# Row transposes one slot later, last roots on VectorE, two expert tiles turned inside the last diffusion tile, some high halves on ScalarE

## The reference

```
a   = layernorm(x)
h   = silu(a @ W_in.T + b_in)
out = term = h
for i in 1..6:                       # diffusion
    term = segment_mean(term[src], dst) / i
    out  = out + term
x1  = x + out @ W_out.T + b_out
xn  = layernorm(x1) * gamma + beta
lg  = xn @ Wr + br                   # 8 logits of a row
w   = softmax(top 2 of lg)
y   = sum over the 2 chosen experts e of
      w_e * (gelu(xn @ W1[e] + b1[e]) @ W2[e] + b2[e])
result = x1 + y
```

## Time and profile before

| | us |
|---|---|
| median of 3 runs (1249.70 to 1251.24) | 1250.63 |
| the profiled execution | 1251.38 |
| its span | 1249.6 |
| sixth step and its row work | 860.1 to 1026.1 |
| expert stage on TensorE | 1029.3 to 1217 |
| TensorE busy in the span | 1154.7 (92%) |
| VectorE, ScalarE, GpSimd busy | 722.2, 414.0, 221.7 |

### The profile page before, as it was taken

One profiled execution on the slowest core, in us unless ns is written; L12 is line 12 of the kernel. 1 busy time (PEld: TensorE's weight loads), 2 busy tenths in 40 slices (PEclk: granted clock), 3 DMA queues, 4 the chain that ended last, 5 costly groups with the idle time before them and its releaser, 6 DMA issues.

```text
span 1249.6 us, 26380 instructions
## 1 busy us (share of the span) xinstructions
PE 1154.7 (92%) x7843; PEld 817.3 (65%) x7843; DVE 722.2 (58%) x1504; ACT 414.0 (33%) x810; POOL 221.7 (18%) x272
## 2 busy tenths in 40 slices
PE   5798999999999999999999999999999977899990
PEld 3586766676566666666666666665666656899980
DVE  7888999993443334442354334442456667866655
ACT  1675665661000000000122111210132227567653
POOL 3000000000112111212000000000022136666750
PEclk8998999999999999999999999999999989999995
DMA  6111010014344334433243123322143232222367
GB/s 158 49 49 30 26 34 30 21 40 104 83 92 111 74 84 99 94 87 64 83 141 109 42 88 98 103 74 32 43 138 113 79 115 76 79 82 91 95 167 214
DMA packets 76860, 105.99 MB, mean 85 GB/s; under 512 B 13472, under 2 KB 62423, under 8 KB 76651
## 3 DMA queue, kind: packets, MB, share of 16 engines
q1 hardware_dynamic: 63044, 72.45, 19.4%
q0 software_dynamic: 11376, 25.55, 9.1%
q10 hardware_dynamic: 2356, 6.93, 2.2%
HBM read 77.00 MB, written 37.49 MB: 92 GB/s over the span
## 4 chain that ended last, share of the span: by engine, by line
PE 78%; DVE 11%; DMA 4%; issue 3%; DVEq 2%; ACT 2%; POOL 1%; ACTq 0%; SPq 0%; POOLq 0%
PE ps L1937 43%; PE ps L1988 8%; PE ps L1915 7%; PE ps L2094 5%; PE ps L2108 5%; PE ps L1883 4%; DVE v_b L1178 4%; PE ps L1851 1%; DMA h_ring<-h_dram 1%; DMA y_dram<-adj,v_a 1%; PE ps L1862 1%; PE ps L2069 1%; DMA adj<-y_dram 1%; DVE adj L1085 1%; PE ps L2031 1%
## 5 line engine op out<-in xcount | busy, mean ns | idle before, releaser
L1937 PE MATMUL ps<-v_a,adj 125*125 125x512 f16 x1375 | 297.3, 379 | 0.0
L1937 PE MATMUL ps<-v_b,adj 125*125 125x512 f16 x1250 | 270.2, 379 | 2.2 <-DVE v_b L1203 2.2
L1937 PEld LDWEIGHTS ps<-v_a,adj 125*125 (+1 forms) x1375 | 187.6, 136 | 109.0
L1937 PEld LDWEIGHTS ps<-v_b,adj 125*125 x1250 | 170.6, 136 | 101.6 <-issue 2.6
L895 ACT ACTIVATE t_hi<-ps,cinv 125x256 f32<-125x256 f32 x125 | 59.2, 474 | 460.1 <-PE ps L1937 404.1
L1185 DVE SCALAR_TENSOR_TENSOR t_hi<-ps,cinv,t_hi 125x256 f32<-125x256 f32 x125 | 60.4, 483 | 240.8 <-ACT t_hi L895 240.8
L1178 DVE TENSOR_TENSOR v_b<-v_b 125x2560 f16<-125x2560 f16 x125 | 180.3, 1488 | 7.7 <-PE ps L1883 7.1
L1988 PE MATMUL ps<-v_b,adj 125*125 125x512 f16 x625 | 143.7, 388 | 3.0 <-DVEq L1371 3.0
L870 ACT ACTIVATE adj<-ps 125x625 f32 (+1 forms) x125 | 112.2, 906 | 67.4 <-PE ps L1883 66.5
L1915 PE MATMUL ps<-v_a,adj 125*125 125x512 f16 x500 | 124.0, 381 | 0.0
L1988 PEld LDWEIGHTS ps<-v_b,adj 125*125 125x125 f16 x625 | 85.4, 140 | 51.5 <-issue 3.7
(11 more groups left out here) (298 smaller groups left out, 1004.4 us busy)
## 6 DMA issues: line engine op xcount, KB each, us to landing
h_ring<-h_dram SPq DMA_DIRECT2D x125, 125.0 KB
v_a<-L_ffn_W SPq DMA_DIRECT2D x32, 256.0 KB, 3.3
v_b<-L_ffn_W SPq DMA_DIRECT2D x32, 256.0 KB, 3.3
adj<-w_dram SPq DMA_DIRECT2D x16, 512.0 KB, 5.4
w_dram<-w_hi SPq DMA_DIRECT2D x32, 128.0 KB, 1.9
hx_dram<-h_dram POOLq DMA_DIRECT2D x25, 125.0 KB, 2.6
hx_dram<-x POOLq DMA_DIRECT2D x25, 125.0 KB, 3.2
hx_dram<-L_gnn_b_out POOLq DMA_DIRECT2D x25, 125.0 KB, 4.1
```

The source lines that it names most:

```text
L1937: last = te.matmul(ps[0:NP, u, :], of_tile(adj[0:NP, 0:ADJ], i, u, a * NP, NP), source[:, a, :], start=(a == 0), stop=(a == T - 1))
```

## The change

It has six parts.

1. Row tiles are transposed on TensorE in slot w+2 in place of w+1, save tiles 10 to 14, which stay; logits follow a slot later on TensorE and on VectorE. Transposes of tiles 23 and 24 and logits of 22 to 24 stand behind the sixth step.
2. TensorE's wait for `term_ok` goes into the untaken branch. Tile 0 waits in its place until 24 of the 25 input tiles are written, and its 25th matmul for the last one.
3. The roots of row tiles 15 to 19 are taken in slot 19, ahead of `place_a`; in slot 20 GpSimd writes the iotas ahead of `add_beta`. Both were in the other order, the roots in slot 20.
4. The roots of tiles 20 to 24 are computed on VectorE alone behind the sixth step (`group_of_itself`, three iterations from an integer first guess), in place of a square root in slot 24 and another for the last tile. The Gelu table is loaded in slot 22.
5. Gathers 0 to 2 are issued in slot 24 ahead of `add_beta` of tile 19; expert tiles 0 and 1 are transposed ahead of matmuls 15 and 20 of the last diffusion tile, and tile 2 behind the hidden part of tile 0. Scaling of row tiles 20 to 24 on ScalarE moves behind Gelu 0 and Gelu 1.
6. For expert tiles 6 to 16 the high half is written by ScalarE behind the Gelu.

```diff
+    HH_TILES = range(6, 17)
...
+        TURN_AT = (T - 10, T - 5)
+        def turn_slot(w):
+            return w + 1 if TA - WIN <= w < TA else w + 2
+        def turned_in(m):
+            return [w for w in range(T) if turn_slot(w) == m]
+        def turn_bank(j):
+            return 2 if j == 0 else (j - 1) % 2
... GpSimd
-                if has(5):
-                    add_beta(m - 5, u)
                 if m == T - 5:
...
+                if m == T - 1:
+                    for r in range(WIN):
+                        pool.wait_ge(xs_out[r], 16 * (TA // WIN))
+                    pool.wait_ge(S["idx_ok"], 1)
+                    for j in range(3):
+                        gather(j)
+                if has(5):
+                    add_beta(m - 5, u)
...
-            for j in range(5):
+            for j in range(3, 5):
                 gather(j)
             add_beta(T - 5, 0)
... ScalarE, the sixth step
-                if m == T - 1:
-                    root_of(NB, WIN - 1)
                 if has(5):
                     normalised(m - 5, u, i)
+                if m == T - 1:
+                    transposed(0)
+                    transposed(1)
...
-                if has(1):
-                    transposed_rows(m - 1)
-                if has(5) and m < T - 1:
+                for w in turned_in(m):
+                    transposed_rows(w)
+                if has(5):
                     high_rows(m - 5, u, i - 1)
...
+                if m == T - 3:
+                    a.activation(gb_max, gb_max, ACT.Gelu)
... ScalarE, expert tile j
                 last.then_inc(S["gelu_ok"], 1)
+                if j in HH_TILES:
+                    act.wait_ge(S["gelu_ok"], j + 1)
+                    need(act, S["ffn_y"], j - FR + 1)
+                    a.activation(h_hi[j % FR]..., h_g[r], ACT.Copy, scale=sh[...]).then_inc(S["hh_ok"], 1)
             def between(j):
                 if j == 0:
-                    normalised(T - 4, 1, NB)
-                    normalised(T - 3, 2, NB)
+                    for k in range(3):
+                        normalised(T - WIN + k, k, NB)
...
-            transposed(0)
-            high_rows(T - 6, 4, NB - 2)
-            normalised(T - 5, 0, NB)
-            act.wait_ge(S["ve_ok"], NB + 1)
-            a.activation(sd3, ve3, ACT.Sqrt).then_inc(S["sd_ok"], 1)
-            transposed(1)
-            a.activation(gb_max, gb_max, ACT.Gelu)
-            transposed_rows(T - 1)
-            transposed(2)
+            transposed_rows(T - 2)
... VectorE
-                if has(3):
-                    logits(m - 3)
-                if has(1):
-                    statistics2(m - 1)
+                for w in turned_in(m - 2):
+                    logits(w)
+                if has(1) and m != T - WIN:
+                    row_statistics(m - 1)
-                if u == 0 and has(WIN):
+                if u == 0 and has(WIN) and m < T - WIN:
                     group_scales(m - WIN, WIN, i)
-                if m == T - 1:
-                    group_scales(T - WIN, WIN - 1, NB)
...
                 if m == T - 6:
+                    row_statistics(m)
+                    group_scales(m + 1 - WIN, WIN, NB - 1)
                     place_a()
...
+            def group_of_itself(t0):
+                group = slice(t0, t0 + WIN)
+                v.tensor_scalar(ve2, mv2[:, group, 1], 1 + 1e-5, 1e-5 ** 2, ALU.mult, ALU.add)
+                v.drain()
+                v.tensor_scalar(root_i, ve2.bitcast(I32), 1, None, ALU.logical_shift_right)
+                v.tensor_scalar(half2, ve2, -0.5, None, ALU.mult)
+                v.drain()
+                v.tensor_scalar(sd2.bitcast(I32), root_i, -1.0, float(0x5f3759df), ALU.mult, ALU.add)
+                v.drain()
+                for _ in range(3):
+                    v.tensor_tensor(rt2, sd2, sd2, ALU.mult)
+                    v.drain()
+                    v.tensor_tensor(rt2, rt2, half2, ALU.mult)
+                    v.drain()
+                    v.scalar_tensor_tensor(sd2, rt2, 1.5, sd2, ALU.add, ALU.mult)
+                    v.drain()
+                group_rows(group, sd2)
... VectorE behind the sixth step
-            statistics2(last)
-            ...
-            logits(last - 2)
+            logits(last - 3)
+            row_statistics(last)
+            group_of_itself(T - WIN)
             low_rows(last - 5, 4)
-            dve.wait_ge(S["sd_ok"], NB + 1)
-            newton(v, sd3, ve3, rt3)
... VectorE, hidden(j)
+                if j in HH_TILES:
+                    dve.wait_ge(S["hh_ok"], HH_TILES.index(j) + 1)
+                else:
+                    dve.wait_ge(S["gelu_ok"], j + 1)
...
-                v.tensor_scalar(hh, h_g[r], sh[:, bass.ds(e, 1)], None, ALU.mult)
-                v.drain()
+                if j not in HH_TILES:
+                    v.tensor_scalar(hh, h_g[r], sh[:, bass.ds(e, 1)], None, ALU.mult)
+                    v.drain()
... TensorE
-            pe.wait_ge(S["term_ok"], 1)
-            pe.wait_ge(S["psum_read"], LAST + 5)
+                pe.wait_ge(S["term_ok"], 1)          # inside the branch that isn't taken
...
                     pe.wait_ge(S["psum_read"], n + 4)
+                    if m == 0:
+                        pe.wait_ge(S["v_ready"], T * STEPS - 1)
                     for a in range(T):
+                        if m == 0 and a == T - 1:
+                            pe.wait_ge(S["v_ready"], T * STEPS)
+                        if m == T - 1 and a in TURN_AT:
+                            transposed(TURN_AT.index(a))
...
-                if has(1):
-                    transposed_rows(m - 1)
+                for w in turned_in(m):
+                    transposed_rows(w)
...
-                if has(2):
-                    logits(m - 2)
+                for w in turned_in(m - 1):
+                    logits(w)
... TensorE, ffn_tiles
-            transposed(0)
+            transposed_rows(T - 2)
...
-    transposed(1)
...
-            if b == 0 and j + 2 < count:
+            if b == 0 and 0 < j < count - 2:
                 transposed(j + 2)
             if j < count:
                 hidden(j, b, *entries[j])
+            if b == steps - 1 and j == 0:
+                transposed(2)
```

## The result

| | before | after |
|---|---|---|
| median, us | 1250.16 (1248.67 to 1251.24) | 1240.83 (1239.4 to 1241.85) |
| ratio, 95% interval | | 0.9921 (0.9908 to 0.9935) |
| span of the profiled execution | 1249.6 | 1239.5 |
| end of step five's matmuls | 857.14 | 858.51 |
| transposes of expert tile 14 | 1079.23 | 1069.17 |

The account below looks back on a forecast made before the run. TensorE was taken to bound the kernel, so only its gaps and clock count. Terms -3.2 -1.1 -2.0 -4.9 -2.6 +0.44 -4.9 +0.7 -1.4 sum to -19.0; from 1251.38 that gives 1232.4, forecast 1232 us, range 1228 to 1240.

Parts of the forecast that it names:

- Seam: Start of the sixth step: 1.6 us idle for the branch's instruction fetch, tile 2 starting 3.2 us earlier.
- the case of a free fetch: At the seam: if the instruction fetch cost nothing, `pool_const` would hold tile 2 at 869.4.
- Tile 6 and the later transposes: Sixth step: later transposes shrink stalls caused by VectorE; after tile 6, 1.39 us becomes 0.3, -1.1.
- Slots 19 to 24: Sixth step: reordered VectorE and GpSimd work gives -2.0 at tile 22, -4.9 at tile 23, -2.6 by full clock.
- Rival (a): Slots 19 to 22: GpSimd's iotas hold VectorE, 2.7 us at most, clock 2.6 more: 1235 to 1237 us; chance 0.10.
- No idle over 2.8 us is left, so tile 23 runs at full clock: -2.6: Tile 23 of the sixth step: without long idles ahead, its matmuls keep full clock, saving 2.6 us.
- Entry and split: Into the expert stage: gathers hidden, first split 6.8 us behind tile 24's end, -4.9 new.
- idle of 3.2: Expert tile 1: TensorE idle from about 1021.5 until VectorE's logits at 1024.7, 3.2 us.
- rival (b): The clock falls anyway, at the seam or in expert tile 1: 1234 to 1237 us; chance 0.12.
- The last line of the ledger: From the first split to expert tile 14: -0.7 us, from +0.7 for Gelu 1 and -1.4 for the high halves.
- the ledger: Forecast against measured gains from step five's end to expert tile 14, line by line: -19.0 forecast, -11.4 measured.
- 1.5 at the seam: Tiles 0 and 1 of the sixth step: 1.5 us lost to low clock before, expected to be regained.

Follow-up runs that it names:

- positions_spread: The changed kernel with two of the three groups of `positions` (20 of 30 narrow matmuls) moved between the matmuls of tile 23: 1263.48 us, 0.9914 of the kernel before.
- early_turns: The changed kernel with rows 0 to 9 transposed one slot earlier, as before the change: 1270.86 us, 0.9956 of the kernel before.
- direct18: The changed kernel with the statistics of row tile 18 written in place, without the small copy: 1235.88 us, 0.9898 of the kernel before.
- betas_wait: The changed kernel with every tile's statistics written in place and GpSimd's work on tiles 15 and 16 behind `place_a`: 1261.04 us, 0.9905 of the kernel before.
- place_positions: `betas_wait` with two of the three groups of `positions` moved between the matmuls of tile 23: 1234.89 us, 0.9877 of the kernel before.
- best3: `place_positions` with logits copies of tiles 22 and 23, gathers 3 to 7 and last weights load earlier, high halves from expert tile 2: 1230.08 us, 0.9843.

## Why the forecast was half right

- **Seam, right in size, wrong in place.** -3.2 forecast, -3.1 measured. The idle of 1.6 us that I had put down to the branch's fetch isn't there (858.51 follows the last matmul at once; two instruction fetches, at 855.89 and 859.60, ran beside matmuls), and `pool_const` holds 1.46, which I had named as the case of a free fetch. By the Trainium skill, "Runtime: NRT & Kernel Launch", section "Instruction fetch mechanics", a taken branch stalls if its target isn't in the fetched window; whether it was, no run shows, and the largest idle at this place in any trace with this seam is 0.21 us (`positions_spread`).
- **Tile 6 and the later transposes**: 1.39 to 0.33, as forecast; `early_turns` shows that without them 1.9 us of the seam's 3.1 would be lost at tile 0's x1.
- **Slots 19 to 24: the failed step.** The sentence "the sum of VectorE's work up to the low half of tile 20 is unchanged, only its waits go" fell. The work moved beside GpSimd's. Rival (a) was this mechanism, priced at 2.7 at most and given 0.10, by the iotas alone. I left out that GpSimd's two-input work on tiles 15 and 16 also moved beside `place_a`, and that VectorE's two-input operations took 0.58 to 0.64 us beside it, for 0.17 to 0.28. `direct18` and `betas_wait` give 1.34 and up to 1.45, so tile 22 came at +0.2 and not at -2.0. The other 2.2 at tile 23 are 1.7 of clock in tile 22, and 0.5 for `positions`: the sum took 2.0 for it, but it took 2.55 (1003.67 to 1006.22), as it had before the change (1008.90 to 1011.44).
- **"No idle over 2.8 us is left, so tile 23 runs at full clock: -2.6"** fell twice. An idle of 3.06 was left, and the clock fell at tile 23 with none ahead of it. Behind 1.48 us of idle in `direct18` it also fell, at 991.6, while before it had not behind 2.77: idle length is not the condition I took it for.
- **Entry and split, right.** The first gather is issued 3.9 us ahead of tile 24's start (1010.03 for 1013.89; 1.2 to 2.8 ahead were forecast), there is no wait for the gathers, and the first split comes 7.1 us behind the end of tile 24 (6.8 forecast).
- **Expert tile 1**: the idle of 3.2 was 4.03, and rival (b) came true, 6.8 us at low clock, so that Gelu 2 was late and VectorE waited 2.23 for it (1034.80). The last line of the ledger, which also has the high halves, is +0.2 for -0.7.
- **Together**, the 7.6 us missing in the ledger are 2.2 at tile 22, whose cause, the contention, is shown; 3.4 of low clock in tiles 22 and 23 (7.30 and 7.26 us for 5.59), measured, though why the clock falls just there is only in part shown; 0.5 for `positions`; and some 1.4 from the first split on, not taken apart. The clock was to give back 4.1 (2.6 at tile 23, 1.5 at the seam) and gave back nothing in sum: 17.0 us low before, 17.0 after. `place_positions`, which removes the contention and spreads `positions` and nothing else, has a stretch of 207.7 where the forecast's was 203.1, as new waits take their place in the entry. `best3` gets to 201.8, but with four more edits.
- **The rivals were priced one at a time.** (a) and (b) came true together. With the added times that I gave them, 3 to 5 and 2 to 5 us, that is 1237 to 1242 (an estimate), and the range ended at 1240.

## What to carry to other kernels

When VectorE work is moved, list what GpSimd does in the same microseconds: here one small copy out of SBUF was held for 1.34 us and operations on two SBUF inputs took two to three times as long, and a chain of them was 2.4 to 2.8 us longer. Count clock falls as a balance and not as a price of one idle time, and over more than one trace; breaking up a block of 30 narrow matmuls kept the clock in slots 21 to 24 in two programs where removing the idle had not in three. Waits in a stage with several lagging engines cover each other: the idle of 4.03 taken out alone gave 1.1, the contention alone 1.1, all the edits together some 9.

## What the runs showed that I had not expected

- A copy of 125 x 2 fp32 on VectorE took 1.51 us beside a GpSimd iota whose row names no input (0.17 alone), in ten traces of ten.
- In three programs the clock fell for 3.4 us behind 30 matmuls of 44 columns, with no idle over 0.45 us in slots 21 to 23.
- Two traces of one program had their first five falls between 300 us and expert tile 8 at the same instructions, and then differed; programs that differ in a few instructions had them elsewhere, and the fall at 317 us stands 540 us ahead of the first instruction that was changed.
- Chips 4 and 15 took 21 to 26 us more than the others in what are 170 us of every kernel elsewhere, while the changed kernel took the same before it, to 2 us, on chip 15 and in the first result; the cause was not looked into.
